# Second cross attention of a two-layer decoder: pieces of four heads of a batch in place of tiles of 128 tokens with all sixteen heads

## The chip, the cores and the metric

One core of one Trainium2 chip runs the whole program. The metric is the device time of one execution in microseconds (us), the median of several runs. The program is a decoder block pair: self attention, cross attention and a feed-forward part, twice, one stage after the other. A barrier over all engines separates the stages.

## The reference, cut to what matters

The change touches the fifth of six steps, the second cross attention. Here x is (4, 512, 128), `ctx_1024` is (4, 32, 128): each of 512 tokens of each of 4 batches attends to 32 keys of its batch with 16 heads of 8 dimensions.

```python
x = x + _L1_xattn_ref(_layernorm(x), ctx_1024, ctx_1024, group_prob, mask, wq_k, wq_b, ...)

def _L1_xattn_ref(query, key_in, value, group_prob, mask, wq_k, wq_b, wk_k, wk_b, wv_k, wv_b, wo_k, wo_b):
    q = _split_heads(query @ wq_k + wq_b, 16)          # (4, 16, 512, 8)
    k = _split_heads(key_in @ wk_k + wk_b, 16)         # (4, 16, 32, 8)
    v = _split_heads(value @ wv_k + wv_b, 16)
    logits = jnp.einsum('bhqd,bhkd->bhqk', q, k) / jnp.sqrt(8.)
    logits = logits + ((1.0 - mask) * -1e9)[:, None, :, :]
    attn = jax.nn.softmax(logits, axis=-1)
    attn = attn * group_prob[:, None, :, :]            # gate after the softmax
    out = jnp.einsum('bhqk,bhkd->bhqd', attn, v)
    return out.transpose(0, 2, 1, 3).reshape(4, 512, 128) @ wo_k + wo_b
```

## The kernel before

Everything is float32. `g.X` holds x in SBUF as 16 tiles of 128 tokens by 128 features (`NT` = 16, four tiles a batch, `SB` = 4). `stage_cross1` (line 1345) is the stage that changes. Each engine has its own program, in program order, and semaphores tie them together; nothing reorders the engines' queues.

**Head.** SyncE loads the four weights, four bias vectors, the mask and the gate (`gp`) at the start of the stage (L1387 to L1393). VectorE (DVE) takes the layer norm's statistics of all 16 tiles (L111, L114), GpSimd (POOL) makes the reciprocal deviations (L120, L122), VectorE writes the normed tiles (L128, 16 instructions). TensorE (PE) turns them (L137), ScalarE (ACT) copies them out (L144), PE projects the queries of a batch (L1434), ACT copies them (L1493). VectorE builds `kd` (L1521): the keys of a batch spread to 16 heads x 32 keys = 512 columns, zero outside the 8 rows of each head. It builds `vd` (L1534), the values in the same manner, and adds the output bias to x (L1540). The loop begins only when all four batches are through all of this.

**Loop.** A step works on one tile of 128 tokens with all 16 heads: 512 logits a token. PE forms the logits of the tile with one product over 128 rows and 512 columns (L1445); VectorE scales, adds the mask (L1550), takes the negated maximum of each head (L1554), adds it (the shift, L1556); ACT takes the exponential (L1498); VectorE sums (L1564) and inverts the sums (L1566); POOL multiplies by the gate (L1413); PE turns the weights in four 128x128 blocks (L1452); ACT copies them (L1503); PE multiplies them with `vd` in four products of 128 columns that add up in one bank (L1462); VectorE divides by the sums (L1573); PE turns the result (L1473). After four tiles ACT copies (L1509), PE multiplies by `wo` (L1480) and VectorE adds to x (L1582). The steps are staggered: in step n an engine works on tile n, on tile n-2, on tile n-3 and so on, and this stagger, written out in each engine's loop, is the order of the work.

A float32 product is run by PE in two passes; the profile counts passes. A transposition is one pass.

## Time and profile before

| | us |
|---|---|
| median of 3 runs | 1184.0 |
| lowest and highest | 1183.9, 1187.14 |
| the profiled execution, its whole time | 1186.93 |
| its span, first to last instruction | 1185.2 |
| `stage_cross1` in it: first statistics to last addition to x | 938.65 to 1023.11 |

The profiled execution is 2.9 us longer than the median. In the profile a row names the engine, the line and the operation, its output and inputs, the shapes, and how often it ran. "Idle before" is the time in which the engine stood still just before such instructions, with the engine and line that ended it. "PEclk" is the granted clock of TensorE as a share of 2.4 GHz: 0.5 is its lower level, 1.2 GHz. Names in the trace lose their buffer numbers: `c_w` is any of the buffers w of this stage.

### The profile page before, as it was taken

To read this page: it belongs to the slowest core of one execution; us is meant where nothing else is said; L and a number is where in the kernel's file an instruction comes from. 1 tells how busy PE (TensorE), PEld (TensorE's weight loads), DVE (VectorE), ACT (ScalarE), POOL (GpSimd) and SP (SyncE) were. 2 spreads that over 40 slices of the span, in tenths; PEclk is the share of its full clock that TensorE was granted. 3 is DMA by queue.
4 is the path that set the end of the run, shared out by engine and by line. 5 is a ranking of instruction groups with operands and counts; after the bars stand their busy time and mean duration, and the time that the engine had idled before them with its cause. 6 is when DMAs were issued, how large, how long until landed. Compare 5 with 4: busy or idle time off the path is not lost. (4 is left out here: it accounts for less than half of the span.)

```text
span 1185.2 us, 20933 instructions
## 1 busy us (share of the span) xinstructions
PE 962.1 (81%) x6175; PEld 495.7 (42%) x6175; DVE 793.7 (67%) x1693; ACT 626.2 (53%) x1548; POOL 355.7 (30%) x533
## 2 busy tenths in 40 slices
PE   4489999999999736899799999999999677352870
PEld 2122233333333134566545555555555435331760
DVE  8789999999999286566556665666656689243111
ACT  4548888888888702222365656656566233110540
POOL 4212222222222131000244454545545423225004
PEclk9759999999999956799899999999999889766995
DMA  1000000000000000000100000000000100105762
GB/s 45 1 1 1 1 2 2 0 0 0 0 0 0 1 15 14 6 16 20 35 14 8 12 10 7 13 7 13 7 8 1 32 0 1 54 1 155 204 188 71
DMA packets 47723, 28.63 MB, mean 24 GB/s; under 512 B 12152, under 2 KB 44208, under 8 KB 47664
## 3 DMA queue, kind: packets, MB, share of 16 engines
q1 hardware_dynamic: 46640, 25.81, 7.9%
q0 software_dynamic: 1024, 2.10, 0.6%
q8 instruction: 29, 0.48, 0.2%
q14 instruction: 30, 0.25, 0.1%
HBM read 22.79 MB, written 5.11 MB: 24 GB/s over the span
## 5 line engine op out<-in xcount | busy, mean ns | idle before, releaser
L509 DVE TENSOR_REDUCE a_nmax<-a_rows 128x2 f32<-128x1024 f32 x256 | 299.2, 1218 | 14.6 <-PE a_rows L415 11.4
L552 ACT ACTIVATE a_probs<-a_turned 128x512 f32<-128x512 f32 x512 | 269.2, 603 | 40.7 <-PE a_turned L437 39.1
L1116 POOL TENSOR_TENSOR a_prob<-a_prob,a_rinv 128x256 f32<-128x256 f32 (+3 forms) x128 | 159.7, 1253 | 173.1 <-DVE a_rinv L1306 172.8
L1299 DVE TENSOR_REDUCE a_nmax<-a_score 128x2 f32<-128x256 f32 (+3 forms) x128 | 105.6, 825 | 124.2 <-PE a_score L1155 119.8
L1253 ACT ACTIVATE a_prob<-a_score,a_nmax 128x128 f32<-128x128 f32 (+3 forms) x256 | 132.7, 523 | 82.4 <-DVE a_nmax L1299 82.0
L437 PE MATMUL a_turned<-a_q,a_qk 32*128 32x512 bf16 x512 | 137.4, 391 | 7.6 <-ACT a_probs L552 5.6
L400 PE MATMUL a_acc<-a_probs,a_vg 128*32 128x512 f32 x1024 | 139.0, 615 | 0.8 <-ACT a_probs L552 0.7
L415 PE MATMUL a_rows<-a_qk 32*128 32x512 bf16 x512 | 111.9, 401 | 13.2 <-DVE a_nmax L509 6.2
L1152 PE MATMUL a_score<-a_k_s,a_q_s 64*128 64x384 f32 (+3 forms) x512 | 103.7, 481 | 2.2 <-ACT a_prob L1253 1.3
L437 PEld LDWEIGHTS a_turned<-a_q,a_qk 32*128 32x128 bf16 x512 | 35.3, 91 | 155.1 <-ACT a_probs L552 131.8
L1312 DVE COPY a_pt<-a_turn 128x128 f32<-128x128 f32 (+3 forms) x224 | 92.2, 447 | 1.4 <-PE a_turn L1166 1.4
L1166 PE MATMUL a_turn<-g_ident,a_prob 128*128 128x128 f32 x640 | 91.8, 274 | 1.0 <-POOL a_prob L1116 0.6
L1179 PE MATMUL a_acc<-a_pt,a_v_s 128*64 128x256 f32 (+3 forms) x512 | 76.0, 439 | 0.8 <-ACT a_pt L1260 0.8
L1166 PEld LDWEIGHTS a_turn<-g_ident,a_prob 128*128 128x128 f32 x640 | 67.9, 141 | 1.7 <-POOL a_prob L1116 1.5
L1152 PEld LDWEIGHTS a_score<-a_k_s,a_q_s 64*128 64x128 f32 x512 | 38.7, 184 | 42.5 <-issue 24.5
L971 ACT ACTIVATE m_silu<-m_gate 128x512 f32<-128x512 f32 x32 | 19.1, 597 | 69.9 <-PE m_up L950 69.9
L1179 PEld LDWEIGHTS a_acc<-a_pt,a_v_s 128*64 128x64 f32 x512 | 34.1, 136 | 49.3 <-issue 43.4
L1253 ACT ACTIVATION_READ_ACCUMULATOR a_prob<-a_score,a_nmax 128x1 f32 x256 | 50.2, 196 | 0.0
L1260 ACT ACTIVATE a_pt<-a_turn 128x512 f32<-128x512 f32 x32 | 19.1, 597 | 47.1 <-PE a_turn L1166 47.1
L936 PEld LDWEIGHTS m_down<-m_wdn,m_hid 128*128 128x128 f32 x256 | 34.7, 198 | 19.7 <-issue 14.9
L415 PEld LDWEIGHTS a_rows<-a_qk 32*128 32x128 bf16 x512 | 24.8, 92 | 41.1 <-DVE a_nmax L509 31.7
L581 POOL COPY a_vg<-t_v_tok 128x64 f32 (+1 forms) x32 | 7.7, 241 | 112.5 <-PE a_acc L400 106.2
(288 smaller groups left out, 1518.9 us busy)
## 6 DMA issues: line engine op xcount, KB each, us to landing
m_w<-L_ffn_w SPq DMA_DIRECT2D x46, 256.0 KB, 3.6
a_wq<-L_attn_Wq SPq DMA_DIRECT2D x16, 128.0 KB, 2.2
xs_sorted<-m_zeros SPq DMA_DIRECT2D x1, 1472.0 KB, 6.6
m_xs<-xs_sorted SPq DMA_DIRECT2D x5, 256.0 KB, 3.6
ys_sorted<-m_ysb SPq DMA_DIRECT2D x5, 256.0 KB, 3.3
g_X<-x SPq DMA_DIRECT2D x4, 256.0 KB, 3.6
m_wgu<-L_ffn_gate_up_proj SPq DMA_DIRECT2D x8, 128.0 KB, 2.1
a_wk<-L_attn_Wk SPq DMA_DIRECT2D x32, 32.0 KB, 2.0
```

The lines of the kernel that those rows point to most:

```text
L400: last = pe.matmul(acc[32 * j:32 * j + 32, :], vg[i % 2][:, tb, j // 2, :], probs[:, (tb % 2) * 4 + j, :], start=(tb == 0 and i % 2 == 0), ...
L415: last = pe.matmul(rows[n % 2][:, jj, :], qk[i % 3][q, 0, sb * P:(sb + 1) * P], qk[i % 3][q, 1, :], start=True, stop=True)
L437: pe.matmul(turned[n % 3][:, :], qk[(i - 1) % 3][q, 1, tb * P:(tb + 1) * P], q2[(i - 1) % 2][q, :], start=True, stop=True).then_inc(turn_i ...
L509: dve.tensor_reduce(nmax[i % 2][:, p // 2, (p % 2) * 2:(p % 2) * 2 + 2], rows[n % 2][:, :, :], AX_X, ALU.max, negate=True).then_inc(row_ou ...
L552: act.activation(probs[:, (tb % 2) * 4 + j, :], turned[n % 3][:, :], ACT.Exp, scale=float(HD0) ** -0.5).then_inc(turn_out, 1)
L1116: pool.tensor_tensor(pr, pr, spread(rinv[:, t % RING, :], 2, width), ALU.mult).then_inc(scl, 1)
L1152: pe.matmul(score[t % 2][:, j, 0:width], q_s[i % 2][p][h, sb * P:(sb + 1) * P], k_s[i % 2][h, 0:width], start=True, stop=False)
L1166: last = pe.transpose(turn[j][:, tb * P:(tb + 1) * P], prob[t % RING][:, j, tb * P:(tb + 1) * P], g.ident[:, :])
L1179: last = pe.matmul(acc[j * HD1:(j + 1) * HD1, tb * P:S], v_s[i % 2][:, tb, :], pt[p][j][:, tb, tb * P:S], start=(tb == 0), stop=(tb == SB ...
L1253: act.activation(prob[t % RING][:, j, 0:width], score[t % 2][:, j, 0:width], ACT.Exp, bias=nmax[:, t % RING, j:j + 1], accum_out=rsum[:, t ...
L1299: dve.tensor_reduce(nmax[:, t % RING, :], score[t % 2][:, :, 0:width], AX_X, ALU.max, negate=True).then_inc(mx, 1)
L1312: dve.tensor_copy(pt[p][j][:, 0:sb + 1, sb * P:(sb + 1) * P], turn[j][:, 0:(sb + 1) * P].rearrange("p (a s) -> p a s", s=P)).then_inc(copi ...
```

## The change

What is computed stays the same. In `stage_cross1`:

- A step of the loop works on a piece: four heads (`HG`) of all 512 tokens of a batch, again 512 logits a partition and again 16 pieces (`PIECES`). The logits are four products over 32 rows (the four heads' 32 features, row group 32 x gr) and 128 columns. The transpositions are four blocks as before. The outputs are four separate products of 32 columns each, which fill a 32-column strip of one shared bank `o`.
- `kd` and `vd` shrink to 128 columns a batch (`kd`) and 4 x 32 (`vd`); the scale is folded into the head mask, so the mask addition is a plain addition of two tensors. `hm4` folds the mask of 16 heads to 4.
- The shift moves from VectorE to GpSimd. The gate writes to buffers of its own, `wg`, and waits for the exponential only.
- The reciprocal and the normalisation run once a batch (64 and 512 elements a partition) instead of once a tile (16 and 128). The same holds for the turning of the result.
- The layer norm of batches 0 and 1 stands ahead of the loop, that of batches 2 and 3 inside it; the turning and projection of batches 1 to 3 are inside it too (tables `STATS`, `NORM`, `TURN`, `PROJ`).
- The addition of the output bias to x moves from VectorE, ahead of the loop, to GpSimd inside it, once a batch.
- PSUM: one bank each for projections, tail and outputs, three for logits, two for transpositions.
- All loads of the stage are issued in the first stage of the program, after the loads of x, `wqkv` and `wo0`, into tiles that live throughout.

```diff
@@ stage_project0, SyncE
+            for n in ("wk", "wv", "wq", "wo"):
+                sp.dma_start(g.c1[n][:, :], dram[f"L1_xattn_{n}_k"]).then_inc(g.c1_in, 16)
...
@@ stage_cross1, GpSimd
-            ln.gpsimd(pool)
-            pool.memset(hmask[:, :], 1.0).then_inc(hm, 1)
+            pool.memset(hmask[:, :], float(HD2) ** -0.5).then_inc(hm, 1)
...
+            ln.gpsimd(pool, (0, 1))
+            for step in range(STEPS):
+                s = step
+                if has(s):
+                    pool.wait_ge(s_nm, s + 1)
+                    pool.tensor_tensor(w[s % 3][:, :, :, :], w[s % 3][:, :, :, :], spread(nmax[:, s % 3, :, :], 3, KEYS),
+                                       ALU.add).then_inc(s_z, 1)
+                s = step - 1
+                if has(s):
+                    b = batch(s)
+                    pool.wait_ge(s_e, s + 1)
+                    wait(pool, s_wt, s - 1)
+                    pool.tensor_tensor(wg[s % 2][:, :, :, :], w[s % 3][:, :, :, :],
+                                       spread(g.c1_gp[:, SB * b:SB * b + SB, :], 2, HG), ALU.mult).then_inc(s_w, 1)
+                if step in STATS:
+                    ln.gpsimd(pool, (STATS[step],))
+                if step % G2 == 0 and 1 <= step // G2 <= B:
...
+                    pool.tensor_tensor(x, x, spread(g.c1["bo"][:, :], 1, SB), ALU.add).then_inc(s_xb, 1)
@@ TensorE
+                for t in range(SB):
+                    last = pe.matmul(logits[s % 3][:, t, :, :].rearrange("p h k -> p (h k)"),
+                                     qt[rows, b, t * P:(t + 1) * P], kd[rows, b].rearrange("p h k -> p (h k)"),
+                                     start=True, stop=True)
...
+                    if gr == 0:
+                        pe.wait_ge(s_vd, 1)
+                        wait(pe, s_on, b)
+                    for t in range(SB):
+                        last = pe.matmul(o_ps[:, t, gr * W2:(gr + 1) * W2], wt[s % 2][:, t, :], vd[:, b, gr, :],
+                                         start=True, stop=True)
@@ ScalarE: in a step the copy of the turned weights (s - 2) stands ahead of the exponential (s)
+                s = step - 2
+                if has(s):
+                    act.wait_ge(s_wt, s + 1)
+                    wait(act, s_o, s - 1)
+                    act.activation(wt[s % 2][:, :, :], turn[s % 2][:, :, :], ACT.Copy).then_inc(s_wtc, 1)
+                s = step
+                if has(s):
+                    act.wait_ge(s_z, s + 1)
+                    act.activation(w[s % 3][:, :, :, :], w[s % 3][:, :, :, :], ACT.Exp).then_inc(s_e, 1)
@@ VectorE, the loop
-                    dve.scalar_tensor_tensor(out=w[k][:, :, :], in0=logits[n % 2][:, :, :],
-                                             scalar=float(HD2) ** -0.5, in1=spread(bias[:, n, :], 1, H2),
-                                             op0=ALU.mult, op1=ALU.add).then_inc(s_l1, 1)
-                    dve.tensor_reduce(nmax[:, k, :], w[k][:, :, :], AX_X, ALU.max, negate=True).then_inc(s_nm, 1)
-                    dve.tensor_tensor(w[k][:, :, :], w[k][:, :, :], spread(nmax[:, k, :], 2, KEYS),
-                                      ALU.add).then_inc(s_z, 1)
...
+                    dve.tensor_tensor(w[s % 3][:, :, :, :], logits[s % 3][:, :, :, :],
+                                      spread(bias[:, SB * b:SB * b + SB, :], 2, HG), ALU.add).then_inc(s_l1, 1)
+                    dve.tensor_reduce(nmax[:, s % 3, :, :], w[s % 3][:, :, :, :], AX_X, ALU.max, negate=True
+                                      ).then_inc(s_nm, 1)
...
+                if step in STATS:
+                    ln.vector_stats(dve, None, (STATS[step],))
+                if step in NORM:
+                    ln.vector_norm(dve, (NORM[step],))
+        STATS, NORM, TURN, PROJ = {1: 2, 5: 3}, {2: 2, 6: 3}, {0: 1, 3: 2, 7: 3}, {1: 1, 4: 2, 8: 3}
```

How the queues read at three places. In these rows c1_ is this stage, the number after a name is the buffer, and x4 is four instructions in a row.

VectorE in the steady loop, one step before:

```order
L1550 SCALAR_TENSOR_TENSOR c1_w0<-c1_logits1,c1_bias 128x512
L1554 TENSOR_REDUCE c1_nmax<-c1_w0 128x16
L1556 TENSOR_TENSOR c1_w0<-c1_w0,c1_nmax 128x512
L1564 TENSOR_REDUCE c1_rsum<-c1_w2 128x16
L1566 RECIPROCAL c1_rsum<-c1_rsum 128x16
L1573 TENSOR_TENSOR c1_on0<-c1_o0,c1_rsum 128x128
```

and at step 7 of the changed loop, where batch 0 closes:

```order
L1581 TENSOR_TENSOR c1_w1<-c1_logits1,c1_bias 128x512
L1584 TENSOR_REDUCE c1_nmax<-c1_w1 128x16
L1592 TENSOR_REDUCE c1_rsum<-c1_w0 128x4x4
L1602 RECIPROCAL c1_rsum<-c1_rsum 128x64
L1606 TENSOR_TENSOR c1_on0<-c1_o,c1_rsum 128x512
L1581 TENSOR_TENSOR c1_w2<-c1_logits2,c1_bias 128x512
```

A step without a closing batch has the first three of these rows alone; the shift is gone from VectorE, and the division stands between the sum of one step and the mask addition of the next.

GpSimd from the end of its head into the loop before:

```order
L1406 MEMSET c1_vd 128x2560
L1409 TENSOR_SCALAR c1_bias<-c1_mask 128x512
L1413 TENSOR_TENSOR c1_w0<-c1_w0,c1_gp 128x512
L1413 TENSOR_TENSOR c1_w1<-c1_w1,c1_gp 128x512
L1413 TENSOR_TENSOR c1_w2<-c1_w2,c1_gp 128x512
```

and at steps 4 to 6 of the changed loop:

```order
L1418 TENSOR_TENSOR c1_w1<-c1_w1,c1_nmax 128x512
L1425 TENSOR_TENSOR c1_wg1<-c1_w0,g_c1_gp 128x512
L1434 TENSOR_TENSOR g_X<-g_X,g_c1_bo 128x512
L1418 TENSOR_TENSOR c1_w2<-c1_w2,c1_nmax 128x512
L1425 TENSOR_TENSOR c1_wg0<-c1_w1,g_c1_gp 128x512
L120 TENSOR_SCALAR c1_ln_ve<-c1_ln_mv 128x4
L122 TENSOR_TENSOR c1_ln_rstd<-c1_ln_ve,g_mhalf 128x4
L1418 TENSOR_TENSOR c1_w0<-c1_w0,c1_nmax 128x512
```

The shift of a piece (L1418) stands ahead of the gate of the piece before it (L1425); the bias addition and the deviations of batch 3 lie between.

TensorE in the steady loop before, one step:

```order
L1445 MATMUL c1_logits0<-c1_kd,c1_qt 128x512
L1452 MATMUL c1_turn0<-g_ident,c1_w1 128x128 x4
L1462 MATMUL c1_o1<-c1_vd,c1_wt1 128x128 x4
L1473 MATMUL c1_ln0<-g_ident,c1_on0 128x128
L1445 MATMUL c1_logits1<-c1_kd,c1_qt 128x512
```

and at steps 7 and 8 of the changed loop:

```order
L1455 MATMUL c1_logits2<-c1_kd,c1_qt 128x128 x4
L137 MATMUL c1_proj<-g_ident,g_XN 128x128 x4
L1484 MATMUL c1_turn1<-g_ident,c1_wg1 128x128 x4
L1496 MATMUL c1_o<-c1_vd,c1_wt0 128x32 x4
L1505 MATMUL c1_tail<-g_ident,c1_on0 128x128 x4
L1455 MATMUL c1_logits0<-c1_kd,c1_qt 128x128 x4
L1445 MATMUL c1_proj<-g_XT,g_c1_wq 128x512
L1484 MATMUL c1_turn0<-g_ident,c1_wg0 128x128 x4
L1496 MATMUL c1_o<-c1_vd,c1_wt1 128x32 x4
L1512 MATMUL c1_tail<-g_c1_wo,c1_ot0 128x128 x4
```

The first outputs of a batch (L1496 in step 7) wait for VectorE's L1606, since the outputs have one bank now; batch 3's layer norm and projection lie in the same two steps as batch 0's tail.

## Rows read from the trace of the kernel before

**Rows 1.** Busy time of PE, PEld, DVE, ACT, POOL by stretch; granted clock; DMA.

```profile
938.00:956.00 18.00, 11.57 (x34) 7.09 (x34) 17.22 (x73) 5.15 (x9) 8.62 (x13) 0.62 0.28 51
956.00:1010.00 54.00, 39.40 (x210) 25.98 (x211) 46.72 (x90) 17.10 (x31) 17.75 (x14) 0.94 0.00 1
```

**Rows 2.** Waits, 938 to 1024 us: who for whom, total us, times, longest.

```profile
POOL c_w L1413 <- DVE c_rsum L1564: 45.1, 15, 13.6
```

**Rows 3.** Groups by line and shape, 900 to 1060 us: busy us, mean ns, idle before.

```profile
L1413 POOL TENSOR_TENSOR c_w<-c_w,c_gp 128x512 f32<-128x512 f32 x16 | 20.3, 1268 | 45.1 <-DVE c_rsum L1564 45.1
...
L1556 DVE TENSOR_TENSOR c_w<-c_w,c_nmax 128x512 f32<-128x512 f32 x16 | 11.1, 692 | 0.6
L1554 DVE TENSOR_REDUCE c_nmax<-c_w 128x16 f32<-128x512 f32 x16 | 11.0, 687 | 0.5
L1550 DVE SCALAR_TENSOR_TENSOR c_w<-c_logits,c_bias 128x512 f32<-128x512 f32 x16 | 10.9, 684 | 5.3 <-PE c_logits L1445 5.3
L1564 DVE TENSOR_REDUCE c_rsum<-c_w 128x16 f32<-128x512 f32 x16 | 10.9, 679 | 0.1
L1498 ACT ACTIVATE c_w<-c_w 128x512 f32<-128x512 f32 x16 | 10.1, 630 | 38.2 <-DVE c_w L1556 38.2
...
L1503 ACT ACTIVATE c_wt<-c_turn 128x512 f32<-128x512 f32 x16 | 9.3, 582 | 4.4 <-PE c_turn L1452 4.4
```

**Rows 4.** Timeline of the stage's head: start us, duration us, what.

```profile
938.65 0.87 DVE L111 BATCH_NORM_STATS2 c_ln_stats<-g_X 128x6 f32<-128x128 f32 x4 [0.94 <-PEq L61]
...
940.20 1.04 POOL L122 TENSOR_TENSOR c_ln_rstd<-c_ln_ve,g_mhalf 128x4 f32<-128x4 f32 x1
...
943.13 6.53 DVE L128 TENSOR_SCALAR g_XN<-g_X,c_ln_mv,c_ln_rstd 128x128 f32<-128x128 f32 x16
...
946.14 2.23 POOL L1406 MEMSET c_vd<- 128x2560 f32 x1
...
950.62 5.01 PE L1434 MATMUL c_ln<-g_XT,c_wq 128*128 128x512 f32 x8
...
954.10 2.50 DVE L1540 TENSOR_TENSOR g_X<-g_X,c_bo 128x512 f32<-128x512 f32 x4
...
957.83 0.69 DVE L1550 SCALAR_TENSOR_TENSOR c_w<-c_logits,c_bias 128x512 f32<-128x512 f32 x1 [1.23 <-PE c_logits L1445]
```

**Rows 5.** GpSimd's groups and one of VectorE's elsewhere in the program.

```profile
L1116 POOL TENSOR_TENSOR a_prob<-a_prob,a_rinv 128x512 f32<-128x512 f32 x32 | 33.3, 1039 | 70.0 <-DVE a_rinv L1306 70.0
...
L607 POOL TENSOR_TENSOR a_o_n<-a_o_tok,a_rsum 128x256 f32<-128x256 f32 x16 | 10.1, 631 | 1.2
...
L658 DVE RECIPROCAL o_rinv<-o_rms 128x64 f32<-128x64 f32 x4 | 2.2, 546 | 0.0
```

**Rows 6.** Timeline of TensorE in the steady loop, one step.

```profile
974.97 0.65 PE L1452 MATMUL c_turn<-g_ident,c_w 128*128 128x128 f32 x4 [1.43 <-POOL c_w L1413]
...
975.46 1.06 PE L1462 MATMUL c_o<-c_vd,c_wt 128*128 128x128 f32 x8
...
976.46 1.02 PE L1445 MATMUL c_logits<-c_kd,c_qt 128*128 128x512 f32 x2
```

**Rows 7.** The tile g_XN's writers in this stage: shortest, median, longest ns.

```profile
L128 DVE TENSOR_SCALAR g_XN<-g_X,c_ln_mv,c_ln_rstd x16: 328/340/2490, 943.1 to 949.3; 128x128 f32<-128x128 f32 x16
```

**Rows 8.** Timeline of the stage's tail.

```profile
1011.98 2.51 POOL L1413 TENSOR_TENSOR c_w<-c_w,c_gp 128x512 f32<-128x512 f32 x2 [2.35 <-DVE c_rsum L1564]
...
1022.42 0.69 DVE L1582 TENSOR_TENSOR g_X<-g_X,c_ln 128x512 f32<-128x512 f32 x1 [2.27 <-PE c_ln L1480]
```

**Rows 9.** Short stretches with the granted clock, columns as in rows 1.

```profile
958.00:962.00 4.00, 1.70 (x4) 0.30 (x2) 3.86 (x7) 0.63 (x1) 0.00 (x0) 1.00 0.00 0
962.00:970.00 8.00, 5.93 (x19) 4.21 (x20) 6.66 (x14) 2.70 (x5) 2.84 (x3) 0.57 0.00 0
970.00:990.00 20.00, 15.93 (x99) 11.01 (x98) 17.56 (x35) 6.23 (x12) 7.30 (x6) 1.00 0.00 1
1056.00:1059.25 3.25, 3.21 (x16) 3.12 (x15) 0.00 (x0) 0.00 (x0) 0.00 (x0) 0.50 0.00 0
```

More of the change, by code:

```diff
@@ L104, in __init__, with vector_stats @@
         self.turned, self.xt = sc.sem("ln_turned"), sc.sem("ln_xt")
[L106 to L107 removed]
+    def vector_stats(self, dve, x_ready=None, batches=range(B)):
+        for b in batches:
             if x_ready is not None:
@@ L114, in vector_stats, with gpsimd @@
                 dve.bn_aggr(self.mv[:, n, :], self.stats[:, n, :]).then_inc(self.aggr, 1)
-    def gpsimd(self, pool):
-        for b in range(B):
+    def gpsimd(self, pool, batches=range(B)):
+        for b in batches:
             t = slice(SB * b, SB * b + SB)
@@ L129, in vector_norm, with tensor @@
                                   self.rstd[:, n:n + 1], ALU.subtract, ALU.mult).then_inc(self.norm, 1)
-    def tensor(self, pe):
-        for b in range(B):
+    def tensor(self, pe, batches=range(B)):
+        for b in batches:
             pe.wait_ge(self.norm, SB * (b + 1))
@@ L139, in tensor, with scalar @@
             last.then_inc(self.turned, 1)
-    def scalar(self, act):
-        for b in range(B):
+    def scalar(self, act, batches=range(B)):
+        for b in batches:
             act.wait_ge(self.turned, b + 1)
@@ L1358, in stage_cross1 @@
+        tail = sc.ps("tail", [P, S])
+        logits = [sc.ps(f"logits{i}", [P, SB, HG, KEYS]) for i in range(3)]
+        turn = [sc.ps(f"turn{i}", [P, SB, P]) for i in range(2)]
+        o_ps = sc.ps("o", [P, SB, D])
+        ln = LayerNorm(sc, g, [proj, proj])
         hmask = sc.sb("hmask", [P, H2])
-        mask = sc.sb("mask", [P, NT, KEYS], I32)
+        hm4 = sc.sb("hm4", [P, HG])
         bias = sc.sb("bias", [P, NT, KEYS])
-        gp = sc.sb("gp", [P, NT, KEYS])
         ctx4 = sc.sb("ctx4", [P, B, 4, KEYS])
-        kt = sc.sb("kt", [P, B * KEYS])
@@ L1405, in _ @@
                                pattern=[[HD2, H2]], channel_multiplier=-1).then_inc(hm, 1)
[L1406 to L1414 removed]
+            pool.memset(vd[:, :, :, :], 0.0).then_inc(vz, 1)
@@ new lines, in _ @@
+            project(0)
+            pe.wait_ge(s_kd, 1)
+            logits_of(0)
+            for step in range(STEPS):
+                if has(step + 1):
+                    logits_of(step + 1)
+                if step in TURN:
+                    turn_rows(TURN[step])
+                if step in PROJ:
+                    project(PROJ[step])
+                s = step - 2
+                if has(s):
+                    pe.wait_ge(s_w, s + 1)
+                    wait(pe, s_wtc, s - 1)
+                    for t in range(SB):
+                        last = pe.transpose(turn[s % 2][:, t, :], wg[s % 2][:, t, :, :].rearrange("p h k -> p (h k)"),
@@ L1478, in _ @@
+                s = step - 4
+                if closes(s):
+                    b = batch(s)
+                    pe.wait_ge(s_on, b + 1)
+                    wait(pe, s_x, b)
+                    for t in range(SB):
+                        last = pe.transpose(tail[:, t * P:(t + 1) * P], on[b % 2][:, t, :], g.ident[:, :])
+                    last.then_inc(s_ot, 1)
+                s = step - 5
+                if closes(s):
+                    b = batch(s)
                     pe.wait_ge(s_otc, b + 1)
-                    for i in range(SB):
-                        last = pe.matmul(ln_ps[b % 2][:, i * P:(i + 1) * P], ot[b % 2][:, i * P:(i + 1) * P],
-                                         wo[:, :], start=True, stop=True)
+                    for t in range(SB):
+                        last = pe.matmul(tail[:, t * P:(t + 1) * P], ot[b % 2][:, t * P:(t + 1) * P], g.c1["wo"][:, :],
+                                         start=True, stop=True)
@@ new lines, in _ @@
+            dve.wait_ge(g.c1_in, 16 * C1_LOADS)
+            for q in range(HG):
+                rows, cols = slice(KEYS * q, KEYS * q + KEYS), slice(q * HD2, (q + 1) * HD2)
+                last = dve.tensor_tensor(vd[rows, :, :, cols], o_ps[rows, :, :].rearrange("p b (a w) -> p b a w", w=W2)[:, :, :, cols],
+                                         spread(g.c1["bv"][rows, :].rearrange("p (a w) -> p a w", w=W2)[:, :, cols], 1, B),
+                                         ALU.add)
+            last.then_inc(s_vd, 1)
```

290 lines of the change are left out of this document (124 added, 166 removed).

## The prediction

> **What bounds the kernel now.** The stage is read in this order: busy time by stretch, waits, groups, then the timeline of head, loop and tail.
>
> By stretch [rows 1] VectorE works 17.2 of 18.0 us in the head and 46.7 of 54.0 us in the loop, PE 39.4, POOL 17.8. The waits [rows 2] say who ends last: POOL's gate stood 45.1 us for VectorE's sum. The groups [rows 3] give VectorE's share of a tile: mask 0.684, maximum 0.687, shift 0.692, sum 0.679, then a reciprocal and a division. So VectorE bounds the loop, with PE not far behind.
>
> The stage runs from 938.65 [rows 4] to 1022.42 + 0.69 = 1023.11 [rows 8], in three parts:
> - head, to the first mask addition at 957.83: 19.2 us. All 16 norms (6.53 us), `kd`, `vd` and four bias additions (2.50 us) stand ahead of it [rows 4];
> - loop, to the end of the last gate at 1011.98 + 2.51 = 1014.49 [rows 8]: 56.7 us;
> - tail, to 1023.11: 8.6 us.
>
> All other stages keep their instructions and queues, so the sum is made on this stage alone.
>
> **Early loads.** Ten more DMAs stand on SyncE's queue in the first stage, behind x, `wqkv` and `wo0`, so nothing that stage needs is queued behind them. The loads of before hide behind the norms. I book the move at nothing by itself; it keeps the shorter head from waiting.
>
> **Head.** New path: VectorE copies `ctx4` (0.4) and takes two batches' statistics. Four took until 943.13, with that copy, so a batch is about 1.03 us: two to 941.1. POOL makes the mask, zeroes a fifth of the old `vd` (2.23 / 5 = 0.45), converts the mask (0.6) and makes the deviations of batch 0 (0.25 + 1.04 [rows 4]); with 0.75 for the head mask it ends at 941.9. Norms of batch 0: 4 x 0.27 (starts of unblocked ones lie that far apart) to 943.1. PE turns four blocks at the lower clock, 1.0; ACT copies, 0.6; PE projects, 1.9 (two passes of 512 columns at 1.2 GHz; the four took 5.01 [rows 4] with the clock rising); ACT copies with a bias, 0.7; eight logit passes at the lower clock, 8 x 0.213 + 0.2 = 1.9. Sum 943.1 + 6.1 = 949.2, with handovers 949.35. VectorE is done with `kd`, norms of batch 1 and `vd` by 945.6, so it waits. Head 10.7 in place of 19.2: **8.5 us less**.
>
> **Loop, by queue.** Price of the shift on POOL: it reads one value for 32 elements. The division L1116 on POOL has that broadcast and costs 1.039 us at 512 elements, L607 with runs of 8 costs 0.631 at 256 [rows 5], so short runs add little. The gate, which repeats a real tensor over heads, costs 1.268 [rows 3]. I take 1.04; 1.27 is the upper bound, 16 x 0.23 = 3.7 us more. The gate stays 1.27. The bias addition on POOL I take as 1.27 (bounds 1.04 and 1.27).
> - POOL: 16 x (1.04 + 1.27) = 37.0, deviations of two batches 2 x 1.35 = 2.7, three of four bias additions 3.8 (the last lies beside the tail). Sum 43.5.
> - VectorE: 16 x (0.684 + 0.687 + 0.679) = 32.8; statistics and norms of two batches 2 x (1.03 + 1.08) = 4.2; three closings, each a reciprocal of 64 (0.546 [rows 5], four of 16 cost four times a fixed part) and a division of 512 from PSUM (0.69, as L1582 [rows 8]); two additions to x inside, 1.4. Sum 42.1.
> - PE per piece: eight logit passes of 128 columns, starts 0.11 apart, 0.86; four transpositions 0.43; eight output passes. The old output group takes 1.06 for eight passes of 128 columns [rows 6]. The new ones stream 32, so between a quarter and the whole of 0.89 from start to start; I take the whole, since each still loads 128 columns of weights. Sum 2.2, plus per batch four transpositions twice, a projection (0.85) and `wo` (0.89), 2.6: about 43 in all.
>
> Of that choice for the output passes: the Trainium skill ("TensorE: Matmul & The Clock Gate", section "LDWEIGHTS (loading the stationary operand)") says that a weight load takes a time that goes by its columns and not by its rows. By that the outputs gain nothing from 32 columns; without it PE would be at 33 us. No row here streams 32 columns, so the trace leaves it open; it is off the sum as long as PE is not last.
>
> So three queues are within 1.5 us of each other, and the loop is longer than any of them by what they make each other wait. POOL's queue is the frame. Laid out step by step from a first shift at 949.35 + 1.4 = 950.8, POOL waits here:
> - steps 0 to 3, 3.5 us: the exponential of piece 1 stands on ACT behind the projection of batch 1 at the lower clock, and the norms of batch 2 (VectorE, step 2) stand between the sum of piece 1 and the mask addition of piece 3, whose shift POOL waits for;
> - step 6 and 7, 0.7: the norms of batch 3, the same way;
> - steps 8 and 12, 1.0 each: reciprocal and division (1.2) stand ahead of the next mask addition; in steady steps VectorE has about 0.4 to spare, since its sum waits for the exponential (0.630), which on ACT stands behind a copy (0.582) [rows 3];
> - step 10, 0.6: PE does batch 0's `wo`, batch 3's projection and the transposition in two steps (3.1 and 3.9 us of work against POOL's 2.3), and ACT's exponential stands behind the copy of the turned weights;
> - handovers and the rest, 0.4.
>
> That is 7.2. The clock adds: between 962 and 970 it was granted at 0.57, after a stretch in which PE was busy 1.70 of 4.00 us [rows 9]. The new loop begins as thinly; I put 1.4 for it. Last gate ends at 950.8 + 43.5 + 7.2 + 1.4 = 1002.9. The loop from its first addition is 53.5 in place of 56.7: **3.2 us less**, far less than the shift (11.1 us busy [rows 3]) that VectorE loses, since its head's work comes back into the loop.
>
> **Tail.** Turn 0.65, copy 0.60, outputs 1.06, division 0.69, turn 0.65, copy 0.60, `wo` 1.06, addition 0.69: 6.0; eight handovers of 0.06 and some of PE at the lower clock: 7.1 in place of 8.6, **1.5 less**. It ends at 1010.0.
>
> **Sum.** 8.5 + 3.2 + 1.5 = 13.2, rounded with its parts to 13. The profiled execution (1186.9, span 1185.2) would be 1173.9. It lay 2.9 above the median of 1184.0; from the median the forecast is **1171.0**.
>
> **The port that two engines share.** Of this stage's 16 norms 15 take about 340 ns and one takes 2490 [rows 7]; it overlaps the memset of 2.23 us on POOL [rows 4]. A norm can thus be held for a POOL instruction's whole length. Eight norms now stand in a loop where POOL is nearly always busy with 1.04 or 1.27 us instructions. Held once a batch, this is in the sum above (step 2). Held at each norm, 8 x 1.2 = 9.6, less the 1.2 already in and the 1.3 that VectorE has spare: 7 more, 1178. For it: the long row. Against it: the norms behind a held one follow each other at 0.27 apart.
>
> The Trainium skill ("SBUF — State Buffer", section "SBUF: two separate sides") says why: VectorE and GpSimd share a port pair as an exclusive lock, held for a whole instruction, against VectorE's instructions in a two-port mode or with two SBUF inputs. By that rule the long norm is no accident, and the trace agrees with 2490 ns.
>
> **The rivals.**
> - *POOL alone sets the loop.* If VectorE's and PE's insertions hide in their spare time, 7.2 shrinks to about 2 and the clock's 1.4 goes: 1171 - 6.6 = 1164. For it: three logits banks and three w buffers. Against it: ACT's fixed order of copy and exponential.
> - *PE or handovers keep the old period.* Loop 56.7 as before: 1174. Any shift price up to 1.27 and a period of 3.5 belong here: 1174 to 1177.
> - *Held norms*, as above: 1178.
> - *The clock stays at its lower level; slower than before.* A piece then costs PE 8 x 0.213 + 4 x 0.213 + 8 x 0.213 = 4.3 and a batch 5.2 more: 16 x 4.3 + 3.5 x 5.2 = 87 in place of 53.5. End 13 earlier turns into 20 later: 1204. It decides when more than 13 / 33 = 0.4 of the loop lies at the lower clock. For it: 32 products with only 8 moving columns, without a pause, were granted 0.50 [rows 9], and the outputs now stream 32 columns and the logits 32 rows. Against it: from 970 on the old loop held 1.00 at 15.9 of 20 us busy, and the new PE is at least as full.
> - *It does not do what it says*: a head gated by late loads. The loads land 900 us earlier; no chance worth a number.
>
> **How the numbers follow.** Forecast 1171: 0.43. POOL alone 1164: 0.17. Old period or dearer shift 1174 to 1177: 0.20. Held norms 1178: 0.08. Lower clock in part (1181 to 1190) 0.06, two thirds of it within 0.3%; throughout (1204) 0.03. Smaller surprises at 1181 to 1184: 0.03. The range is 1163 to 1180. About 0.3%, 3.6 us, is what a measurement can tell from no change. Faster by more, below 1180.4: 0.88. Within: 0.07. Slower: 0.05.
>
> **What would show it.** Right: first mask addition about 10.7 us into the stage; POOL busy over 0.8 of the loop, its shift near 1.04; VectorE waiting for ACT's exponential before sums; a stage of 71 us. Wrong: a shift near 1.27; norms of over 1 us in the loop; logits rows of VectorE waiting for PE all along; a granted clock under 0.8 over the loop.

## The result and the profile after

| | before | after |
|---|---|---|
| median, us | 1183.95 (4 runs, 1177.16 to 1187.14) | 1200.05 (4 runs, 1193.77 to 1204.18) |
| ratio of the two, 95% interval | | 1.0139, 1.0071 to 1.0207 |
| profiled execution; its span | 1186.93; 1185.2 | 1193.77; 1192.1 |
| head: VectorE's first instruction of the stage to the first mask addition | 19.2 | 11.4 |
| loop: to the end of the last gate | 56.7 | 72.6 |
| tail: to the end of the last addition to x | 8.6 | 13.0 |
| stage | 84.5 | 97.0 |

The change costs 16 us where 13 less was forecast. The stage is 12.5 us longer in the profiled executions, of which that of after is the fastest of its four. The head became 7.8 us shorter, where 8.5 was forecast; the loop and the tail became longer, by more than they were to gain. (VectorE's first instruction of the stage is the first statistics before, 938.65, and the copy of `ctx4` after, 935.59; from the first statistics the head of after is 11.1.)

Outside the stage the instructions are the same, and yet that part of a profiled execution varies, from 1094.7 to 1107.5 us over the fourteen traces of this case, most of it in the first stage; so the stage's own length is a sharper measure than a median of four executions.

The stretches of the kernel after, in the columns of [rows 1]:

```profile
945.00:950.00 5.00, 5.00 (x25) 4.44 (x26) 2.66 (x4) 0.98 (x2) 1.21 (x2) 0.50 0.00 0
...
975.00:980.00 5.00, 5.00 (x24) 4.71 (x23) 3.59 (x7) 1.11 (x2) 2.27 (x2) 0.50 0.00 0
980.00:985.00 5.00, 5.00 (x24) 4.67 (x23) 1.21 (x2) 2.31 (x4) 3.54 (x3) 0.50 0.00 0
985.00:990.00 5.00, 5.00 (x25) 3.64 (x23) 1.91 (x3) 1.80 (x3) 1.53 (x2) 0.66 0.01 2
990.00:995.00 5.00, 5.00 (x42) 4.60 (x41) 4.07 (x7) 1.73 (x4) 2.98 (x3) 1.00 0.02 3
995.00:1000.00 5.00, 5.00 (x25) 4.74 (x25) 4.02 (x7) 1.62 (x3) 3.48 (x5) 0.52 0.00 0
1000.00:1005.00 5.00, 5.00 (x24) 4.45 (x22) 1.58 (x3) 1.71 (x3) 3.27 (x3) 0.50 0.00 0
...
947.02:1019.60 72.58, 71.78 (x319) 62.39 (x318) 42.67 (x80) 21.77 (x38) 42.59 (x40) 0.55 0.00 1
```

The last row is the loop. PE is busy for 71.8 of 72.6 us, and its granted clock is 0.55, where the old loop had 0.94 [rows 1]. It is 0.50, the lower level of 1.2 GHz, nearly everywhere; in the one stretch at 1.00 PE gets through 42 records in 5 us, in the others shown through 24 or 25. The groups of the kernel after, 930 to 1040 us, in the columns of [rows 3]:

```profile
L1455 PE MATMUL c_logits<-c_kd,c_qt 32*128 32x128 f32 x128 | 30.1, 416 | 0.9 <-ACT c_qt L1520 0.9
...
L1496 PE MATMUL c_o<-c_vd,c_wt 128*128 128x32 f32 x128 | 24.6, 352 | 0.8 <-DVE c_on L1606 0.8
L1425 POOL TENSOR_TENSOR c_wg<-c_w,g_c_gp 128x512 f32<-128x512 f32 x16 | 20.3, 1266 | 4.5 <-ACT c_w L1542 4.5
L1418 POOL TENSOR_TENSOR c_w<-c_w,c_nmax 128x512 f32<-128x512 f32 x16 | 16.7, 1046 | 31.5 <-DVE c_nmax L1584 31.5
L1484 PE MATMUL c_turn<-g_ident,c_wg 128*128 128x128 f32 x64 | 16.6, 411 | 0.0
...
L1581 DVE TENSOR_TENSOR c_w<-c_logits,c_bias 128x512 f32<-128x512 f32 x16 | 11.0, 686 | 15.8 <-PE c_logits L1455 15.7
...
L1434 POOL TENSOR_TENSOR g_X<-g_X,g_c_bo 128x512 f32<-128x512 f32 x4 | 5.0, 1262 | 0.0
```

Its waits, same stretch, in the columns of [rows 2]:

```profile
ACT c_wt L1538 <- PE c_turn L1484: 32.7, 16, 5.3
POOL c_w L1418 <- DVE c_nmax L1584: 31.5, 14, 8.2
DVE c_w L1581 <- PE c_logits L1455: 15.7, 9, 4.2
```

POOL, which was to set the pace, waits 31.5 us for VectorE's maxima, VectorE waits 15.7 for PE's logits, ACT 32.7 for PE's turned weights, and PE is idle for 0.8 us of the loop's 72.6. PE is the bound. The timeline of two pieces shows at what cost (start, duration, what):

```profile
977.00 2.07 PE L1455 MATMUL c_logits<-c_kd,c_qt 32*128 32x128 f32 x8
...
979.91 1.06 PE L1484 MATMUL c_turn<-g_ident,c_wg 128*128 128x128 f32 x4
...
980.77 1.75 PE L1496 MATMUL c_o<-c_vd,c_wt 128*128 128x32 f32 x8
...
990.12 1.15 PE L1455 MATMUL c_logits<-c_kd,c_qt 32*128 32x128 f32 x8
...
991.21 0.66 PE L1484 MATMUL c_turn<-g_ident,c_wg 128*128 128x128 f32 x4
...
991.71 0.98 PE L1496 MATMUL c_o<-c_vd,c_wt 128*128 128x32 f32 x8
...
992.61 1.15 PE L1455 MATMUL c_logits<-c_kd,c_qt 32*128 32x128 f32 x8
...
995.10 1.97 PE L1455 MATMUL c_logits<-c_kd,c_qt 32*128 32x128 f32 x8
```

At the lower level a piece's logits, turns and outputs take 2.07, 1.06 and 1.75 (4.4 from start to start without the insertion between them; the instructions overlap); at the upper one 2.49, from 990.12 to 992.61. Even there it is more than the 2.2 of the forecast. Just ahead of the rise stand the two 512-column passes of batch 3's projection (L1445 at 985.36); after it PE runs one more set of outputs, the `wo` of batch 0 and two pieces of 32-row and 32-column products without a pause, and falls back. The same two passes ran for batches 1 and 2 (from 950.91 and 963.41) without a rise, so they are not shown to be its cause.

### The profile page after: what moved, and what is told of

Same layout as the page of the kernel before. It is cut to its first block and busy times, and to the rows that moved or that the text cites. A ratio compares the mean times of both kernels' runs of the same rounds, so it can differ in the third digit from the quotient of the medians.

```text
span 1192.1 us, 21067 instructions
## 1 busy us (share of the span) xinstructions
PE 987.4 (83%) x6271; PEld 529.9 (44%) x6271; DVE 775.2 (65%) x1635; ACT 625.9 (53%) x1548; POOL 374.6 (31%) x553
## 3 DMA queue, kind: packets, MB, share of 16 engines
q0 software_dynamic: 1024, 2.10, 0.6%
## 5 line engine op out<-in xcount | busy, mean ns | idle before, releaser
L518 DVE TENSOR_REDUCE a_nmax<-a_rows 128x2 f32<-128x1024 f32 x256 | 299.1, 1216 | 14.6 <-PE a_rows L424 11.3
L980 ACT ACTIVATE m_silu<-m_gate 128x512 f32<-128x512 f32 x32 | 19.1, 597 | 67.1 <-PE m_up L959 67.1
L1269 ACT ACTIVATE a_pt<-a_turn 128x512 f32<-128x512 f32 x32 | 19.1, 597 | 47.2 <-PE a_turn L1175 47.2
```

The source lines that it names most:

```text
L518: dve.tensor_reduce(nmax[i % 2][:, p // 2, (p % 2) * 2:(p % 2) * 2 + 2], rows[n % 2][:, :, :], AX_X, ALU.max, negate=True).then_inc(row_ou ...
```

## The experiments

All stage times are of the profiled executions and in the parts of the table above. The stage starts somewhere between 935 and 947 us, depending on the clock granted in the unchanged stages ahead of it, so its own length is told beside the median. Each ratio goes by the executions of the kernel before that were measured together with that kernel; parts, stage and clock come from one trace each, and those of b2, b3 and e4 are of the slowest execution.

| kernel | median | ratio to before, 95% | head | loop | tail | stage | clock in the loop |
|---|---|---|---|---|---|---|---|
| before | 1184 to 1186 | | 19.2 | 56.7 | 8.6 | 84.5 | 0.94 |
| after | 1200.1 | 1.0139 (1.0071 to 1.0207) | 11.4 | 72.6 | 13.0 | 97.0 | 0.55 |
| e1_rows128 | 1181.2 | 0.9961 (0.9928 to 0.9994) | 11.4 | 54.0 | 15.2 | 80.7 | 0.88 |
| e2_cols128 | 1177.3 | 0.9931 (0.9897 to 0.9966) | 11.0 | 59.9 | 10.6 | 81.4 | 0.79 |
| e3_both128 | 1172.3 | 0.9882 (0.9825 to 0.9938) | 11.0 | 54.1 | 8.7 | 73.9 | 0.93 |
| e3c_flags | 1178.4 | 0.9939 (0.9895 to 0.9983) | 11.0 | 54.0 | 8.7 | 73.7 | 0.93 |
| b1_cols32 | 1189.7 | 1.0053 (1.0019 to 1.0087) | 19.1 | 60.4 | 10.2 | 89.6 | 0.81 |
| b2_rows32 | 1190.0 | 1.0051 (1.0001 to 1.01) | 18.0 | 62.4 | 7.0 | 87.4 | 0.78 |
| e4_filler | 1203.7 | 1.0171 (1.0123 to 1.0219) | 11.9 | 83.6 | 13.7 | 109.3 | 0.50 |
| e7_filler4 | 1185.4 | 1.0018 (0.9996 to 1.0041) | 11.9 | 63.0 | 11.3 | 86.1 | 0.87 |
| e5_shift_dve | 1182.7 | 0.9988 (0.9945 to 1.003) | 11.0 | 61.1 | 11.7 | 83.8 | 0.83 |
| e8_two_o | 1170.3 | 0.9894 (0.9848 to 0.9939) | 11.0 | 50.6 | 7.6 | 69.2 | 0.93 |
| b3_early | 1183.6 | 0.9972 (0.9952 to 0.9992) | 18.9 | 56.0 | 7.0 | 82.0 | 0.97 |
| b4_shift_pool | 1180.4 | 0.995 (0.9931 to 0.9968) | 19.2 | 52.9 | 8.6 | 80.7 | 0.97 |

### What the products stream: e1, e2, e3

The theory: the changed logits (32 rows of the array in place of 128) and the changed outputs (32 columns in place of 128) are what holds the clock down, though PE never pauses. The rival: PE at the lower clock is a matter of the new order or of the higher load, and wide products would suffer alike. Each kernel is the change with one or both products made wide again, at the same number of products. The wide `kd` and `vd` hold zeros where the narrow ones had nothing; VectorE builds the wide `kd` in four instructions in place of one, and POOL zeroes the wide `vd` behind the deviations. The heads of 11.0 and 11.4 show that this costs nothing there.

e1_rows128, logits over 128 rows:

```diff
-                                     qt[rows, b, t * P:(t + 1) * P], kd[rows, b].rearrange("p h k -> p (h k)"),
+                                     qt[:, b, t * P:(t + 1) * P],
+                                     kd[:, b, HG * gr:HG * gr + HG, :].rearrange("p h k -> p (h k)"),
```

> The changed kernel, but each logits product reads all 128 rows (the keys of a batch spread to 16 heads, as before), 128 columns as in the change. PE has as many passes as in the change. In the profile of the change the granted clock was 0.50 in 13 of 15 stretches of 5 us from 945 to 1020 us, with PE never idle, and the stage took 97.0 us. Theory A (the 32-row logits hold the clock down): the granted clock rises over 0.9 in the loop and the stage falls to 71 to 76 us, the kernel to 1171 to 1178. Theory B (the 32-column outputs hold it down): no difference, clock near 0.5, stage 95 to 98. Theory C (either is enough, both must go): as B.

e2_cols128, outputs of 128 columns that add up over the four pieces of a batch:

```diff
-                        last = pe.matmul(o_ps[:, t, gr * W2:(gr + 1) * W2], wt[s % 2][:, t, :], vd[:, b, gr, :],
-                                         start=True, stop=True)
+                        last = pe.matmul(o_ps[:, t, :], wt[s % 2][:, t, :], vd[:, b, gr * P:(gr + 1) * P],
+                                         start=(gr == 0), stop=(gr == G2 - 1), skip_group_check=True)
```

> The changed kernel, but each output product streams 128 columns that add up over the four pieces of a batch, as before, in place of 32 columns. The number of passes stays. Theory A (32-row logits are the cause): clock near 0.5, stage 95 to 98 us or a little more, since at the lower clock a pass of 128 columns takes no longer than its weight load. Theory B (32-column outputs are the cause): clock over 0.9, stage 71 to 76 us. Theory C: as A.

e3_both128 is both edits together.

> Both: logits over 128 rows and outputs of 128 columns in the changed loop. Theory A, B and C (narrow products hold the clock down) all give a granted clock over 0.9 in the loop and a stage of 71 to 76 us, the forecast of before the result. Theory D (it is the order of the loop or its thin start that leaves the clock down, not the shapes): clock near 0.5 and a stage of 95 us or more in all three kernels.

In e2 and e3 the output is off by 0.07 (relative), because each tile's first product opens a sum in the one bank that they share; by the order of the products, three of the four tiles' sums would lose their first piece. The instructions and their shapes are as written, so their times stand; e3c_flags below has the full sums.

Measured: loops of 54.0, 59.9 and 54.1 in place of 72.6, stages 16.3, 15.6 and 23.1 shorter than the change's. None of the theories A, B and C had this for e1 and e2: each expected either nearly all or nothing of one wide product, and each of the two brings about two thirds of the stage's 23.1. What all three had for e3 came true (clock 0.93, stage 73.9), and D, by which the order holds the clock down, is out. The stretches of e3_both128:

```profile
945.00:950.00 5.00, 5.00 (x33) 4.52 (x32) 3.76 (x8) 1.79 (x3) 2.37 (x3) 0.82 0.00 0
950.00:955.00 5.00, 1.83 (x15) 1.45 (x13) 4.96 (x14) 1.86 (x4) 4.43 (x5) 1.00 0.00 0
...
970.00:975.00 5.00, 3.04 (x14) 3.07 (x15) 3.59 (x6) 1.23 (x4) 4.06 (x4) 0.57 0.01 2
...
980.00:985.00 5.00, 5.00 (x47) 5.00 (x46) 4.48 (x8) 2.23 (x4) 3.44 (x4) 1.00 0.02 3
...
990.00:995.00 5.00, 5.00 (x48) 5.00 (x47) 4.38 (x8) 2.17 (x4) 4.90 (x5) 1.00 0.00 0
```

With the same 128 passes each of logits and outputs, but wide, PE is granted 1.00 in most stretches. It falls to 0.57 from 970 to 975, where PE is busy for 3.04 of 5.00, and is back at 1.00 by 980. From e3's timeline at 1.00:

```profile
980.02 1.06 PE L1454 MATMUL c_logits<-c_kd,c_qt 128*128 128x128 f32 x8
980.91 0.60 PE L1484 MATMUL c_turn<-g_ident,c_wg 128*128 128x128 f32 x4
981.35 1.06 PE L1496 MATMUL c_o<-c_vd,c_wt 128*128 128x128 f32 x8
982.24 1.06 PE L1454 MATMUL c_logits<-c_kd,c_qt 128*128 128x128 f32 x8
```

A wide piece takes 2.22 from start to start, a narrow one at the same clock 2.49. The difference is not in the passes, which start 0.11 apart in both; it lies around the 32-row logits, whose group takes 1.09 from its start to that of the turns (992.61 to 993.70) in place of 0.89. Why is not shown. Over 16 pieces that is 4.3 us of PE's time in e3's favour that the clock has no part in; e3's PE is busy for 43.0 of 54.1, so little of it need show in the loop. The rest, from 2.49 to 4.4 a piece, is the clock's. Either product alone, made wide, brings most of the loss back; both are needed for 0.93. e1's tail of 15.2 is where its narrow outputs run without the wide logits between them; its clock there is 0.50.

### Only one sum opened in the bank: e3c

```diff
-                                         start=(gr == 0), stop=(gr == G2 - 1), skip_group_check=True)
+                                         start=(gr == 0 and t == 0), stop=(gr == G2 - 1), skip_group_check=True)
```

> Logits over 128 rows and outputs of 128 columns in the changed loop, as in e3_both128, where the first product of each of the four column blocks of the output bank opened its sum; here only the very first product of a batch in the bank does. All theories: the same time as e3_both128, 1172 within 3 us, stage 73 to 75 us. The question of this run is which of the two ways of opening the sums keeps the earlier pieces' part.

The stage is that of e3 within 0.2 us (73.7), and the output is the reference's. The median, 1178.4, lies 6 above e3's, where 3 at most were expected. The profiled executions, 8.3 us apart, show where: e3c starts the stage 10.0 us later, and all of that has arisen in the first stage, whose instructions are the same (its first 100 us ran at 0.74 in e3c and at 0.85 in e3). Why the clock differs there is open; this stage has no part in it.

### Narrow products in the old loop: b1, b2

The same in the other direction, on the kernel before. b1_cols32 leaves all as it is but for the outputs' columns:

```diff
-                        last = pe.matmul(o_ps[n % 2][:, 0, :], wt[n % 2][:, a, :], vd[:, b, a * P:(a + 1) * P],
-                                         start=(a == 0), stop=(a == TURNS - 1))
+                        last = pe.matmul(o_ps[n % 2][:, 0, 32 * a:32 * a + 32], wt[n % 2][:, a, :],
+                                         vd[:, b, 160 * a:160 * a + 32], start=True, stop=True)
```

> The kernel before, with one part of the change alone: the four output products of a tile stream 32 columns each into their own strip, in place of 128 columns that add up. Theory B: the clock falls in the old loop too and it becomes 1190 or slower. Theory A: loop clock as before, 0.94 from 956 to 1010 us, time within 0.3% of before. Theory D: as A.

b2_rows32 forms the logits from 32 rows, at 512 columns; the logits of the other heads are left out, so its output is not the reference's:

```diff
-                    pe.matmul(logits[n % 2][:, :, :].rearrange("p h k -> p (h k)"), qt[:, b, t * P:(t + 1) * P],
-                              kd[:, b, :], start=True, stop=True).then_inc(s_lg, 1)
+                    r = slice(32 * (n % 4), 32 * (n % 4) + 32)
+                    pe.matmul(logits[n % 2][:, :, :].rearrange("p h k -> p (h k)"), qt[r, b, t * P:(t + 1) * P],
+                              kd[r, b, :], start=True, stop=True).then_inc(s_lg, 1)
```

> The kernel before, with the logits of a tile taken from 32 rows in place of 128 (the other heads' logits are left out, so its output differs); the product still streams 512 columns. The counterpart of b1_cols32, which took the outputs alone and came out 0.5% slower. Theory E: the clock falls in parts of the old loop, and the kernel is 0.3 to 1.5% slower. Rival: 512 columns are enough to keep the clock whatever the rows, time within 0.3% of before.

b1's loop falls from 0.94 to 0.81 and takes 3.7 more; b2's falls to 0.78 and takes 5.8 more. The kernels are 0.5% slower each, the interval of b2 only just without 1 (1.0001). First b1, then b2:

```profile
990.00:995.00 5.00, 5.00 (x19) 3.86 (x19) 2.91 (x5) 0.65 (x2) 0.94 (x1) 0.50 0.00 0
```

```profile
980.00:985.00 5.00, 5.00 (x17) 3.17 (x16) 3.09 (x7) 1.12 (x2) 1.26 (x1) 0.50 0.00 0
```

Stretches with PE busy for 5.00 of 5.00 at 0.50 are to be had in the old order as well, by narrowing one product. That excludes the new order as the cause. In neither kernel does the clock stay down throughout; each has one kind of wide product left.

Narrow shapes alone do not bring the clock down, though. The unchanged first stage consists largely of them, and has 1.00; in the kernel before, from 300 to 400 us:

```profile
300.00:400.00 100.00, 94.89 (x728) 29.58 (x729) 89.81 (x85) 87.99 (x175) 23.58 (x73) 1.00 0.00 0
```

From its timeline:

```profile
300.45 1.07 PE L400 MATMUL a_acc<-a_probs,a_vg 128*32 128x512 f32 x8
301.45 0.39 PE L437 MATMUL a_turned<-a_q,a_qk 32*128 32x512 bf16 x1
301.45 0.39 PE L415 MATMUL a_rows<-a_qk 32*128 32x512 bf16 x2
```

There the products hold 32 columns (L400) or 32 rows (L437, L415) of the array, but they stream 512 columns, and several run at once: eight passes of 512 columns in 1.07 us, where two take 1.02 in the loop before [rows 6]. Which of the two differences keeps the clock up was not tested.

### Wide products added to the change: e4, e7

To tell what is streamed from how much is run: the change plus one further product a piece, whose result is overwritten unread, and then plus four.

```diff
+                    pe.matmul(turn[s % 2][:, :, :].rearrange("p t k -> p (t k)"), g.ident16[:, :], fill[:, :],
+                              start=True, stop=True)
                     pe.wait_ge(s_w, s + 1)
                     for t in range(SB):
                         last = pe.transpose(turn[s % 2][:, t, :], wg[...
```

`fill` is a bfloat16 tile of 128x512 ones. e7_filler4 has the product in a loop of four. In the expectations, E is the theory by which fuller products bring the clock back, F the one by which they only add their time.

> The changed kernel with its narrow products as they are, plus one product of 128 rows and 512 columns in bfloat16 a piece, whose result is overwritten: 16 more, 0.21 us each at 2.4 GHz and 0.43 at 1.2. Theory E (the granted clock follows how much of the array the products use, and the narrow ones leave it down): the clock rises over parts of the loop, and the kernel becomes faster by adding work: 1180 to 1193. Theory F (a narrow product keeps the clock down whatever runs beside it): the clock stays near 0.5 and the loop grows by 16 x 0.43 = 7 us, kernel 1200 to 1207.

> e4_filler stayed at 0.50 in every stretch. Here four such products a piece in place of one, on top of the change's narrow products: 64 products of 128 rows and 512 columns, 0.21 us each at 2.4 GHz and 0.43 at 1.2. Theory E (the clock follows how fully the array is used, and one was too little): the clock rises, a piece costs PE about 2.2 + 0.6 + 0.85 = 3.7 us, the loop falls from 72.6 us to 60 to 68, and the kernel gets faster than the change by adding 64 products. Theory F (narrow products keep the clock down whatever runs beside them): clock near 0.5, loop 72.6 + 16 x 1.7 = 100 us, kernel 1215 or more.

One a piece brought nothing: the loop grew by 11.0 to 83.6 (F had 7) at a clock of 0.50 in every stretch, as F had it. Four a piece, 64 more products than the change has, made the loop 9.6 shorter than the change's and the kernel 15 faster, at 1185.4. The stretches of e7_filler4:

```profile
955.00:960.00 5.00, 5.00 (x19) 3.70 (x19) 3.80 (x8) 1.11 (x2) 2.61 (x3) 0.50 0.00 0
960.00:965.00 5.00, 5.00 (x27) 3.75 (x26) 1.60 (x4) 1.71 (x3) 1.93 (x2) 0.73 0.01 3
965.00:970.00 5.00, 4.84 (x31) 3.41 (x32) 2.88 (x12) 1.80 (x3) 3.89 (x4) 1.00 0.00 0
...
1010.00:1015.00 5.00, 5.00 (x40) 4.26 (x38) 1.15 (x2) 1.67 (x3) 0.90 (x1) 1.00 0.00 0
```

More work on a saturated engine and less time: that is the clock, 0.87 in place of 0.55. It speaks against a cap by load, and for the content of the stream. e4 alone would have pointed the other way. The added products differ from the kernel's own in type, columns and rows at once, so how much of each counts is not settled.

### The other parts of the change, one at a time: e5, b3, b4

e5_shift_dve is e3c with the shift back on VectorE, behind the maximum. b4_shift_pool is the kernel before with the shift on POOL and the gate's own buffers `wg`, in the change's order (shift of n ahead of gate of n-1). b3_early is the kernel before with the change's early loads alone.

```diff
# e5_shift_dve
-                    pool.wait_ge(s_nm, s + 1)
-                    pool.tensor_tensor(w[s % 3][:, :, :, :], w[s % 3][:, :, :, :], spread(nmax[:, s % 3, :, :], 3, KEYS),
+                    dve.wait_ge(s_nm, s + 1)
+                    dve.tensor_tensor(w[s % 3][:, :, :, :], w[s % 3][:, :, :, :], spread(nmax[:, s % 3, :, :], 3, KEYS),
                                       ALU.add).then_inc(s_z, 1)
# b4_shift_pool
+                shift(n)
+                if n:
+                    gate(n - 1)
-                    dve.tensor_tensor(w[k][:, :, :], w[k][:, :, :], spread(nmax[:, k, :], 2, KEYS),
-                                      ALU.add).then_inc(s_z, 1)
# b3_early
@@ stage_project0, SyncE
+            for n in ("wk", "wv", "wq", "wo"):
+                sp.dma_start(g.c1[n][:, :], dram[f"L1_xattn_{n}_k"]).then_inc(g.c1_in, 16)
```

> e3c_flags with the shift back on VectorE. VectorE's queue grows by 16 x 0.69 = 11 us to 53, GpSimd's falls by 16.7. If the three queues are near each other, as the forecast said, VectorE becomes the bound and the loop grows by 4 to 8 us: 1176 to 1181. Rival: GpSimd was the bound and each piece's chain gets shorter, 0.69 in place of 1.05: 1168 to 1172.

> The kernel before with the change's early loads alone. The forecast booked them at nothing: time within 0.3% of before, stage 84 to 85 us. Rival: ScalarE's copy of the keys waited for the bias load until 944.95 in the kernel before, and the head gets up to 2 us shorter.

> The kernel before with the shift on GpSimd alone, and gates into buffers of their own; tiles, head and tail as before. VectorE's share of a tile falls from 3.24 to 2.55 us, GpSimd's rises to 2.32, PE's stays at 2.5 with its wide products. If VectorE's queue bounds the old loop, it falls from 56.7 us to 47 to 50, the stage to 75 to 78, the kernel to 1175 to 1178. Rival: the longer chain of a tile (maximum, shift on GpSimd, exponential, sum) gives it back, loop 53 to 57.

e5: with VectorE's 11 us back, the loop takes 61.1 in place of 54.0, and part of it is again the clock's (0.83): PE waited more (for `c_on`, 9.7) and dropped after the waits. VectorE is busy for 55.0 of the 61.1. b4: the loop goes from 56.7 to 52.9, where I had expected 47 to 50; two waits stand in its place:

```profile
ACT c_w L1512 <- POOL c_w L1414: 35.2, 16, 4.0
...
PEld c_turn L1466 <- POOL c_wg L1420: 24.8, 14, 4.1
```

No queue is full in that loop (VectorE busy for 39.4 of 52.9, PE for 38.9, POOL for 36.4), so it is a chain that binds, by these waits the one of a piece through two POOL instructions, one of them behind another piece's gate. The rival had it so; no further run tests it. Measured alone, the shift's move is worth 0.5% of the kernel. b3: the head is 18.9 against 19.2, so the loads had hardly held it up, though ACT's copy of the keys now comes 0.6 us into the stage in place of 6.3. The stage is 2.5 shorter (82.0), which I had not expected; 1.6 of it is the tail, which ran at 1.00 in this trace and at 0.81 in that of before. One trace each does not show whether the loads have a part in that. The kernel's 0.3% (0.9972, up to 0.9992) is at the edge of what can be told.

### A second bank for the outputs: e8

e3 and e3c waited for the one bank of outputs: the first outputs of a batch stand behind VectorE's division of the batch before. From the timeline of e3_both128:

```profile
971.13 0.69 DVE L1605 TENSOR_TENSOR c_on<-c_o,c_rsum 128x512 f32<-128x512 f32 x1
...
971.96 1.41 PE L1496 MATMUL c_o<-c_vd,c_wt 128*128 128x128 f32 x5 [2.15 <-DVE c_on L1605]
```

e8_two_o is e3c with two banks of outputs, and two of logits in place of three:

```diff
+        o_ps = [sc.ps(f"o{i}", [P, SB, D]) for i in range(2)]
-                wait(pe, s_l1, s - 2)
+                wait(pe, s_l1, s - 1)
-                        wait(pe, s_on, b)
+                        wait(pe, s_on, b - 1)
-                        last = pe.matmul(o_ps[:, t, :], wt[s % 2][:, t, :], vd[:, b, gr * P:(gr + 1) * P],
+                        last = pe.matmul(o_ps[b % 2][:, t, :], wt[s % 2][:, t, :], vd[:, b, gr * P:(gr + 1) * P],
```

> e3c_flags with two banks for the outputs and two for the logits, in place of one and three. In e3_both128 PE waited 4.6 us for the division (three times) because the outputs have one bank. If that wait is on the path the loop falls from 54 to 51 to 53 us. Rival: the third logits bank was worth as much, and the loop stays at 54 or grows.

The loop is 50.6 against 54.0 at the same clock of 0.93, the tail 7.6, the stage 69.2: 15.3 less than before the change. The wait for the bank is gone:

```profile
L1496 PE MATMUL c_o<-c_vd,c_wt 128*128 128x128 f32 x128 | 17.7, 285 | 0.0
```

The stage is the shortest of all. The kernel takes 1170.3, 1.1% less than before; by the ratios to before it cannot be told from e3 (0.9894 and 0.9882). A third bank of logits was worth less than a second one of outputs.

## Why the prediction was wrong, point by point

- **The step that failed is the dismissal of the clock rival**, and with it the price of PE. The "Sum 2.2" for a piece took its products at the upper level. The rival's price was close: 4.3 us a piece, measured 4.4; 1204 for the kernel, measured 1200. The reason against it was that "the new PE is at least as full" as the old one, which had been granted 1.00 at 15.9 of 20 us busy. PE was fuller, 71.8 of 72.6, and was granted 0.55. Busy share was the wrong quantity: e3 at the same counts of passes had 0.93, e7 with more had 0.87. The row that pointed the right way was there: [rows 9], where products of 8 columns without a pause had 0.50. I gave it as evidence and let an average over other shapes overrule it, at 0.03 for "throughout". What it is about the narrow products that keeps the clock down (rows, columns, or how many run at once) stays open. Two of the signs of "wrong" came: a clock under 0.8 over the loop, and VectorE's mask additions waiting for PE.
- **The logits' price was too low at the upper level as well**: 0.86 a piece, taken from 128-row products; 32-row ones take 1.09. With 2.49 in place of 2.2 a piece PE's queue would have been about 47.6 and not 43, and so the longest of the three.
- The Trainium skill ("TensorE: Matmul & The Clock Gate", section "What's actually happening") has a busy TensorE at 2.4 GHz. By that the loop of after would be at 1.00 and near the 53.5 forecast. The rows of after show 72.6 at 0.55 with PE busy throughout; the measurement decides.
- **Loop, 72.6 against the rival's 87.** A granted clock of 0.547 over 72.6 us means 6.8 us at the upper level, around 988 to 995, which saved about as much. The turns of the last two pieces and the outputs of the last three, 2 x 0.9 + 3 x 1.6 = 6.6, lie behind the last gate, in the tail. That leaves 74.
- **Tail, 7.1 forecast, 13.0.** It is mostly PE, at a clock of 0.63: at 1.2 GHz outputs take 1.75, turns 1.1, `wo` 2.06 to 2.08. In e3 the same tail is 8.7, so 1.6 of the 5.9 was missed for another reason. When e3's last gate ends, at 999.9, PE still has the outputs of three pieces and batch 2's `wo` ahead of the last turn of the result; I had priced one set of outputs.
- **Head, 10.7 forecast, 11.4**, 11.0 in e3. Right in the main: batches 2 and 3 out of the head, kept, at 11.0 to 11.9, by all nine kernels that have it. It is the one gain that the clock could not take back.
- **Early loads at nothing**: borne out for the head (b3, 0.2 us shorter); the rest of b3's stage leaves it open.
- **The shift's price on POOL, 1.04, bound 1.27**: right, 1.046. The bias addition 1.26 against 1.27, the reciprocal 0.543 against 0.546. The prices from rows of the same shape and pattern were all good.
- **POOL sets the loop, 53.5**: near once PE is at the upper level, and in part by luck. e3's loop is 54.1 with POOL busy for 42.4, and at 4.90 or 5.00 of 5.00 in its densest stretches. But the waits were not those I priced: PE stood 4.6 us for the bank of outputs, which the sum held no price for. e8 without it comes to 50.6, between the forecast and the rival of POOL alone.
- **Outputs at the price of 128 columns, whole**: right. Eight passes of 32 columns take 0.90 from start to start at the upper level (991.71 to 992.61), of 128 columns 0.89 in e3; the rule on weight loads that the prediction cited agrees.
- **Norms held once a batch**: right for the kernel after, where the first norm of batch 2 takes 0.90 and that of batch 3 1.05, and the others 0.34. In e3 two of batch 2's four are held, 1.07 and 1.30 beside two POOL instructions, and the four take 2.80; held at each they would have taken 4 x 0.34 + 4 x 1.2. The reading of [rows 7] was off: of the 16 norms before, three are long (2490, 2300 and 715 ns), all in the one hold during the memset.

```profile
965.85 2.80 DVE L128 TENSOR_SCALAR g_XN<-g_X,c_ln_mv,c_ln_rstd 128x128 f32<-128x128 f32 x4 [1.20 <-POOL c_ln_rstd L122]
```

Summed, with wide products the change takes 73.9 us for the stage, forecast 71, and 1172 (e3) to 1178 (e3c) for the kernel, forecast 1171. With the narrow ones that it has, the loop lost 18.5, the tail 4.3 and the head 0.4 against e3: 23.1 us for products that do the same work in the same number of passes.
